# Transposed scores of a 16-head attention: a 32-row contraction in row quarters of the array instead of a zero-padded 128-row one

## The reference, cut to what matters

```python
def _L1_attn_ref(x, w_qkv, w_proj, b_proj):      # x: 16, 512, 128
    qkv = (x @ w_qkv).reshape(B, L, 3, H, D).transpose(2, 0, 3, 1, 4)   # H = 16, D = 8
    q, k, v = (qkv[0], qkv[1], qkv[2])
    q = _apply_rope(q, cos, sin)
    k = _apply_rope(k, cos, sin)
    attn = jnp.einsum('bhqd,bhkd->bhqk', q, k) * scale
    attn = jax.nn.softmax(attn, axis=-1)
    out = jnp.einsum('bhqk,bhkd->bhqd', attn, v)
    out = out.transpose(0, 2, 1, 3).reshape(B, L, C)
    return out @ w_proj + b_proj
```

## Time and profile before

| what | value |
|---|---|
| median of 3 executions | 2734.68 us |
| lowest, highest | 2734.5, 2736.84 us |
| the profiled execution's own time | 2733.82 us |
| its span, first to last instruction | 2732.0 us |
| mean granted TensorE clock over the span | 0.929 of full |
| TensorE matmuls, busy | 2360.9 us (86%) |
| VectorE, busy | 2036.4 us (75%) |
| ScalarE, busy | 1376.8 us (50%) |
| GpSimd, busy | 927.3 us (34%) |
| first and last reduction L1487 | 1184.0, 2283.3 us |
| first value matmul L1904 | 1207.7 us |

### The profile page before, as it was taken

The page is one execution under the profiler, slowest core; times in us unless marked ns, Lnnn a source line. Parts: engine busy times, 40 slices in busy tenths (PEclk is TensorE's granted clock), DMA queues, the critical chain, the costliest instruction groups (busy, mean ns, idle before and its releaser), DMA issues.

```text
span 2732.0 us, 39397 instructions
## 1 busy us (share of the span) xinstructions
PE 2360.9 (86%) x11490; PEld 1609.2 (59%) x11490; DVE 2036.4 (75%) x4734; ACT 1376.8 (50%) x2035; POOL 927.3 (34%) x836
## 2 busy tenths in 40 slices
PE   4498576679499999879999999999999997899999
PEld 3376355557377777635555555555555554778777
DVE  6587677568499999757777777777777774788887
ACT  0187222168344444336656565656566664444444
POOL 6500665400377777511111111111111100465554
PEclk9999555589699999969999999999999999999999
DMA  6343110044388888600000000000000000888887
GB/s 160 108 139 100 32 36 27 27 153 141 84 169 174 188 174 175 149 16 16 17 15 16 16 16 15 15 14 16 16 16 16 15 16 7 177 179 178 184 182 158
DMA packets 122741, 228.94 MB, mean 84 GB/s; under 512 B 19475, under 2 KB 22550, under 8 KB 122246
## 3 DMA queue, kind: packets, MB, share of 16 engines
q1 hardware_dynamic: 114214, 210.47, 33.7%
q0 software_dynamic: 8416, 17.25, 2.4%
HBM read 184.13 MB, written 28.85 MB: 78 GB/s over the span
## 4 chain that ended last, share of the span: by engine, by line
PE 61%; DVE 14%; ACT 7%; issue 7%; DMA 6%; POOL 4%; POOLq 1%; SPq 1%; DVEq 0%; ACTq 0%
PE ps L1880 11%; PE ps L1904 9%; PE ps L1607 7%; PE ps L1609 6%; PE ps L1608 6%; PE ps L1891 6%; DMA gate_rows<-gates_dram 4%; DVE m L1324 2%; POOL sorted_x L653 2%; ACT g L786 2%; PE ps L1621 1%; ACT g_hi L759 1%; PE ps L1953 1%; DVE shift L1487 1%; ACT xnT_hl L759 1%
## 5 line engine op out<-in xcount | busy, mean ns | idle before, releaser
L1487 DVE TENSOR_REDUCE shift<-ps 128x1 fp32r<-128x512 f32 x1024 | 671.5, 685 | 142.2 <-PE ps L1880 135.2
L914 ACT ACTIVATE prob<-ps 128x1024 f32<-128x1024 f32 x512 | 524.9, 1026 | 378.1 <-PE ps L1891 374.2
L759 ACT ACTIVATE hi<-m 128x512 fp32r<-128x512 f32 x512 | 318.9, 632 | 415.1 <-DVE m L1324 414.9
L605 POOL TENSOR_TENSOR lo<-m,hi 128x512 fp32r<-128x512 f32 x256 | 342.2, 1339 | 308.0 <-ACT hi L759 307.7
L1880 PE MATMUL ps<-k_pad,q_st 128*128 128x512 f32 x1024 | 406.4, 438 | 29.7 <-DVE shift L1487 28.8
L1324 DVE SCALAR_TENSOR_TENSOR m<-ps,gate_rows 128x512 f32<-128x512 f32 x512 | 334.6, 679 | 90.3 <-DMA gate_rows<-gates_dram 45.7
L1880 PEld LDWEIGHTS ps<-k_pad,q_st 128*128 128x128 f32 x1024 | 179.7, 190 | 293.2 <-DVE shift L1487 263.6
L1891 PE MATMUL ps<-q_sh,k_pad 128*128 128x512 f32 x1024 | 331.3, 405 | 0.0
L1904 PE MATMUL ps<-prob,v_cols 128*32 128x512 f32 x2048 | 272.8, 605 | 0.4 <-ACT prob L914 0.4
L1006 DVE TENSOR_TENSOR lo<-m,hi 128x512 fp32r<-128x512 f32 x256 | 208.4, 814 | 16.9
L1607 PE MATMUL ps<-hi,vals_hl 128*128 128x512 f32 x512 | 209.7, 410 | 0.9 <-POOL lo L605 0.9
(11 more groups left out here) (223 smaller groups left out, 4230.3 us busy)
## 6 DMA issues: line engine op xcount, KB each, us to landing
gate_rows<-gates_dram SPq DMA_DIRECT2D x256, 512.0 KB, 12.2
w_blk<-w_dram SPq DMA_DIRECT2D x38, 514.5 KB, 3.7
k_pad<-k_st SPq DMA_DIRECT2D x256, 64.0 KB, 2.0
x_blk<-sorted_x SPq DMA_DIRECT2D x38, 256.0 KB, 3.5
sorted_y<-yb_rows SPq DMA_DIRECT2D x38, 256.0 KB, 2.0
out<-x SPq DMA_DIRECT2D x16, 256.0 KB, 17.1
x<-in_x SPq DMA_DIRECT2D x1, 2560.0 KB, 14.2
w_dram<-in_W SPq DMA_DIRECT2D x8, 256.0 KB
```

The lines of the kernel that those rows point to most:

```text
L605: pool.tensor_tensor(m["lo"][:, s], m["m32"][:, s], m["hi"][:, s].bitcast(F32), ALU.subtract).then_inc(sig(ph, "lo_pool"), 1)
L759: return act.activation(o, i, ACT.Copy)
L914: act.activation(prob[:, h % HP, 2 * half:2 * half + 2, :], ps[:, b0:b0 + 2, :], ACT.Exp, scale=SCALE).then_inc(sig(ph, "prob"), 1)
L1487: dve.tensor_reduce(shift[:, g % 2, b, c:c + 1], wide(PASS1 + b % 2), AXX, ALU.max, negate=True).then_inc(sig(ph, "qmax"), 1)
```

## The change

Pass 2 no longer reads the padded keys. For head j it takes rows 32j to 32j+31 of the stacked keys `k_st` as the stationary operand (32 rows x 128 columns) and the same rows of `q_sh` as the moving one, so each matmul sits in one row quarter of the array; `pass2(t, h, 0)` uses quarters 0 and 1, `pass2(t, h, 1)` quarters 2 and 3. Count, columns, order and PSUM banks of the matmuls stay. Since pass 2 now reads `k_st` long after the DMAs, `k_st` keeps all four groups (two more buffers of 512 columns), and the room comes from `qk_hl`, which has one buffer in place of two. Pass 1 and the DMAs into `k_pad` stay.

```diff
-        qk_hl = [late_sb(f"qk_hl{b}", [P, 2, 2, SEQ], F32R) for b in range(2)]
+        qk_hl = [late_sb("qk_hl", [P, 2, 2, SEQ], F32R)] * 2
         k_pad = late_sb("k_pad", [P, HEADS, SEQ], F32R)
-        k_st = late_sb("k_st", [P, 2, SEQ], F32R)
+        k_st = late_sb("k_st", [P, GROUPS, SEQ], F32R)
...
-                    sp.dma_start(k_pad[r, HPG * g + j, :].bitcast(F32), k_st[r, g % 2, :].bitcast(F32)).then_inc(sig(4, "k_pad"), 16)
+                    sp.dma_start(k_pad[r, HPG * g + j, :].bitcast(F32), k_st[r, g, :].bitcast(F32)).then_inc(sig(4, "k_pad"), 16)
...
-                    act.activation(k_st[:, g % 2, :], wide(MISC), ACT.Identity, bias=one_row)\
+                    act.activation(k_st[:, g, :], wide(MISC), ACT.Identity, bias=one_row)\
...
                     for j in (2 * half, 2 * half + 1):
-                        last = pe.matmul(wide(PASS2 + j), k_pad[:, HPG * g + j, kb * P:kb * P + P],
-                                         q_sh[:, g % 2], start=True, stop=True)
+                        last = pe.matmul(wide(PASS2 + j), k_st[rows(j), g, kb * P:kb * P + P],
+                                         q_sh[rows(j), g % 2], start=True, stop=True)
```

## The result

The changed kernel took 2807.35 us, median of 4 executions (2796.79 to 2810.12), against 2734.59 us; the ratio is 1.0257, 95% interval 1.023 to 1.0285. In a later session it was 1.0247 (1.0221 to 1.0274). It is slower, as forecast, by 71 to 73 us where 55 were expected. Some 57 of them are the visits to the row quarters that the prediction priced; the other 14 to 16, by the medians, come with TensorE's clock.

A forecast was written before the change was run, and what follows sets the result against it. TensorE was taken to bound the attention stage; 346 exposed pass-2 pairs at 0.16 us more each gave 55 us, other terms 0, so 2789 us from the profiled 2733.8. The range was 2745 to 2845 us.

The forecast's parts named there:

- What bounds: Attention stage: TensorE alone bounds the quick steps; a second pair's delay moves the whole ring; 346 exposed pairs.
- Quick steps: Six of a tile's 16 steps between value-matmul groups, TensorE never idle: 3.5 us each, forecast 3.8.
- steps with a wait: Ten of a tile's 16 steps, 4.9 us each, TensorE waiting for VectorE after the first pair: forecast 0.16 us longer.
- the counts 96 and 250: Exposed first pairs (6 of 16 steps) and second pairs (all 16 steps) in the stage, at 0.16 us each.
- The pair's price: Two pass-2 heads side by side in row quarters, entering and leaving included: 0.85 against 0.69, 0.16 us more a pair.
- Cover: First pairs of the steps with a wait: the wait for VectorE hides them, cost 0; without it 26 us more.
- Memory and DMAs at 0: Four groups of `k_st`, `k_pad`, its 256 DMAs and one `qk_hl` buffer: no new wait, cost 0.
- ScalarE at 0: Exponentials after a pass-2 pair start some 0.1 us later; ScalarE busy 7.07 of 10.50 us: cost 0.
- The rival of the free mode: Row quarters entered and left without a price: pair 0.24 instead of 0.46, -76 us, 2658 us; chance 0.13.
- The clock: Rival: TensorE's clock falls in the attention stage, quick steps nearly double, over 600 us; chance 0.02.
- the forecast mechanism: Pass-2 pairs pay for entering and leaving row quarters, 0.12 to 0.20 us a pair: 2775 to 2803 us, chance 0.57.
- loads in turn: Rival: second head's 128-column load waits for the first's, 0.27 a pair, 93 us, 2827 us; chance 0.15.

The follow-up runs named there:

- the two half changes: Changed kernel with row quarters for heads 0 and 1 only, or heads 2 and 3 only, the others on padded keys: 2747.58 us (1.0065) and 2775.61 us (1.0153).
- the kernel with the memory part alone: Changed kernel, but pass 2 still takes the padded keys; four groups of stacked keys and one `qk_hl` buffer stay: 2731.87 us, ratio 0.9998.
- pass 2 alone in one visit: Changed kernel with both pass-2 pairs put together, ahead of pass 1's blocks 2 and 3, and ScalarE's key-stack copies later: 2704.19 us, ratio 0.9898.

## Why the prediction was right, and where it was short

**What bounds.** Right. Quick steps, in which TensorE alone bounds, took the full loss; steps with a wait took half of it. The forecast of 3.8 us against 3.84 and the 0.16 a slow step against 0.17 are the two readings that carry the sum, and the two half changes put 15 and 43 us where the counts 96 and 250 at 0.16 say 15 and 40.

**The pair's price.** Right in each term: 0.32 in, both heads side by side, 0.43 for load, stream and the way out (0.42 forecast), 0.11 for the next open load. (The forecast also names the second full matmul's own 0.23; its 0.85 and 0.69 both leave that out, so the difference stands.) It came from rows of another mode, the four column quarters of the values, and a single 3-row matmul at half clock. The Trainium skill's rule (TensorEngine Tiling (Array Packing), Key Properties) that a change of the tiling mode drains TensorE holds here, with about 0.1 us each way; the two open loads, which that sentence doesn't speak of, cost 0.11 each, as much again.

**Cover.** Right: 44.50 us for nine slow steps with the first pair in quarters, 44.40 without.

**Memory and DMAs at 0.** Right, by the kernel with the memory part alone. ScalarE at 0 was not tried by itself; the visits came to 57 where 55 were forecast, so little is left for it.

**The rival of the free mode** was wrong: every visit pays its way in and out. What the prediction set beside it, matmuls of different quarters starting nearly together, is of matmuls inside the mode, and that holds: four heads in a visit do stream together, and that version is 1% faster than before. What decides is how many matmuls a visit carries. A visit takes 0.62 us of TensorE by the forecast's terms (0.09 in, 0.11 for its load, 0.01 between heads, 0.21 streaming, 0.09 out, 0.11 for the open load behind); the rows say 0.63, with 0.43 for the middle four. At 0.23 for a full matmul two heads lose by it and four win.

**The clock** is the step that failed. The prediction put it at nothing in the sum and gave it 2 in 100, because "TensorE stays busy as often as before". That was true, busy 38.27 of 39.40 us in the first six steps, and it didn't help: the clock rose 39 us later (1242.5 instead of 1203.7). The sum was short by 16 to 18 us. The late rise, with the short falls, makes 14 to 16 of them, and 2 lie in the visits, 57 where 55 were forecast. My price for that rival, over 600 us, was that of a stage wholly at half clock. It came near only in the two versions with both passes in quarters (516 and 577 us over before). That the time still fell into the range is partly luck. It lies just above the 2775 to 2803 of the forecast mechanism, in the part that was kept for loads in turn, and the rows exclude those (two heads fill 0.50 us, four 0.51).

That the later falls matter little is argued from their 3.4 us each, not tried. Why one execution in four was quicker stays open, and so does what the clock answers to: the runs show with which placements it stays low, not why.

## What to carry to other kernels

Before packing small matmuls into row quarters, count the visits, not the matmuls: here a visit cost 0.62 us whether it carried two heads or four, so four matmuls of 0.23 gain and two lose. Put what can share the quarters next to each other first, and look which visits lie under a wait. Then look at the granted clock of every stage, since TensorE that is busy all the time in quarters may run at 1.2 GHz, as it did here for 539 us.

## What the runs showed of the hardware that I had not expected

TensorE busy 98% of 539 us stood at clock 0.50, while the same score work over 128 rows, busy 93%, had 0.99. The clock fell more with more of the score matmuls in row quarters: pass 2 alone in two visits a step, a late rise and falls of 3.4 us; pass 2 alone in one visit, a rise 1.8 us behind the first value matmul where it was 4 ahead before, and no fall; pass 1 alone, long stretches; both, most of the stage. The seven short falls, and the long stretch at half with pass 1 alone, began within 2 us of a pause. The Trainium skill (TensorE: Matmul & The Clock Gate, Part 1) says that the gate's ratio follows how busy the engine has been; by the busy time that these rows count, that doesn't foretell it.

Four matmuls in four row quarters, each with a load of 128 columns, took together no longer than two (0.51 and 0.50 us in their rows), and the loads of all four filled 0.19 us, as one load does.
